# The gated delta-rule stage of a decoder kernel: gating and output projection in the next slot, late formings on two pairs of banks, compactions between exponentials

## The chip, the cores and the metric

The kernel runs as one program on one core of a Trainium2 chip. A core has TensorE (PE; its weight loads are PEld), VectorE (DVE), ScalarE (ACT), GpSimd (POOL) and SyncE (SP), each with its own instruction queue, which it works through in order; they meet through semaphores. TensorE writes PSUM, eight banks of 512 floats on 128 partitions. The metric is the time of the whole kernel in microseconds on the device.

## The reference

A decoder of four layers over x of 16 sequences, 128 tokens, 256 channels. All the change touches is the first sublayer: a gated delta rule with 8 heads, each in 8 modes, key and value width 64.

```python
q, k, v = (x @ Wq), (x @ Wk), (x @ Wv)              # 8 heads of 64
beta, tg = sigmoid(x @ Wbeta), sigmoid(x @ Wtg)     # one per head and mode
g = log(clip(tg * rho, 1e-6))                       # rho from log_decay
# q and k are rotated, with frequencies per head and mode, and normalised
def step(S, (q_t, k_t, v_t, b_g, b_beta)):          # over the 128 tokens
    S = S * exp(b_g)
    dv = (v_t - k_t S) * b_beta
    S = S + k_t^T dv
    return S, q_t S
o = sum over modes of softmax(mode_logits) * step outputs
o = o * sigmoid(x @ Wg)
x = layernorm(x + o @ Wo)
```

## The kernel before

The stage is `delta_stage`. A **slot** g is one of the 16 sequences. It has two **units**, u = 2g (heads 0 to 3, hf 0) and u + 1 (heads 4 to 7, hf 1). A unit is 32 combinations of head and mode, in eight groups of four. The recurrence is solved in matrix form: decayed products of keys with keys and queries (`NB`, 128 x 128 for each combination), the inverses of their 32 x 32 diagonal blocks, and three block couplings.

The steps of a unit, by function:

- *Rotation* (`rotate`, VectorE, two multiplications for each half; `add_halves`, GpSimd) makes `kq` for a pack of two groups.
- *Exponents* (`phase`, TensorE, in bank 0), *exponential* (`decays`, ScalarE, into `NB`), *products* (`phase`, TensorE, banks 4 and 5 for even groups, 1 and 2 for odd), *multiplication* (`take_products`, VectorE). These run over eight groups: "the phase of a unit".
- *Compaction* (`take_lower`, ScalarE): the diagonal blocks of `NB` into `diagonal`. *Inversion* (`invert`, VectorE): a transposition, 60 small dependent operations, a transposition. In gaps between these operations other steps of VectorE are put, by a list of positions. *Spreading* (`spread`, ScalarE): the inverses into the block diagonal `Df`.
- *Forming* (`form`, TensorE, banks 6 and 7) multiplies a group of `NB` by `Df`; `take_formed` (ScalarE, four copies) takes it back. Eight a unit: two of them inside the next unit's phase, six after it. *Identities* (`set_identities`, ScalarE) prepare the next unit's diagonal blocks.
- *Couplings* (`couple`, q = 1, 2, 3; four heads each, 16 small matmuls a head, into banks 4 to 7) and *solutions* (`solutions`, ScalarE); *output* (`output`, TensorE, bank 3).
- *Gating* (`gated`, VectorE) multiplies the output of a unit by the gates of the slot; after both, the *output projection* (`project_out`, TensorE, bank 3) and, in the next slot, sum and normalisation (`finish`, `applied`).

Each engine's order is written out by hand in its `turn(g, ...)`: slot 0 and slot 15 straight, slots 1 to 14 as a hardware loop (`Fori`). A slot's queue on each engine goes: phase of the odd unit with the first formings of the even one; late formings, couplings and output of the even unit, with the q, k, beta and decay projections of slot g + 1 in between; phase of the next slot's even unit; late formings, couplings and output of the odd unit, with the v projection and the gates' projection of slot g + 1. In VectorE's queue gating stands ahead of the phase:

```python
invert(u + 1, between(*sorted(steps, key=lambda x: x[0])))
gated(g, 0)
if more:
    phase(g + 1, u + 2, 0)
    invert(u + 2)
gated(g, 1)
```

After this stage come eleven others, which the change leaves alone.

## Time and profile before

| | |
|---|---|
| median of 3 runs | 6994.44 us (6984.17 to 7002.9) |
| the profiled execution, its own time | 7007.31 us |
| its span in the trace | 7005.5 us |
| granted TensorE clock, mean | 0.836 of full |
| delta-rule stage | 0 to about 2605 us of the span |
| the 14 middle slots | about 153.5 us each, some 157 |

In the rows below a timeline line is: start in us, duration in us, engine, line of the code, operation, what it writes and reads, how many instructions are merged in it, and in brackets the idle time of the engine before it with what ended it ("issue": nothing that the profile shows). A windows line is: the stretch, its length, the busy us of PE, PEld, DVE, ACT and POOL with the number of instructions, the granted clock as a share of 2.4 GHz, the share of DMA, GB/s.

### The profile page before, as it was taken

What the parts mean: (1) busy time and instruction counts of PE and PEld (TensorE: products, weight loads), DVE (VectorE), ACT (ScalarE), POOL (GpSimd) and SP (SyncE); (2) the same over time, 40 slices, a digit from 0 to 9 for tenths busy, and PEclk for the clock granted to TensorE, in tenths of its full rate; (3) what the DMA queues carried; (4) which work ended last, traced back from release to release, by engine and by line L of the source; (5) the groups of instructions that cost most, each with busy time, mean ns of one, the idle gap of its engine ahead of it and who ended that gap; (6) DMA issues with size and microseconds to landing.
All of it is one profiled execution on the core that took longest, in us unless ns stands there. A gap on an engine that the chain in (4) does not pass through costs nothing. (4 is left out here: it accounts for less than half of the span.)

```text
span 7005.5 us, 79394 instructions
## 1 busy us (share of the span) xinstructions
PE 5363.7 (77%) x28132; PEld 3704.0 (53%) x28132; DVE 3454.2 (49%) x7576; ACT 2207.6 (32%) x3719; POOL 1034.3 (15%) x845
## 2 busy tenths in 40 slices
PE   3778778777777775899998877547768567788698
PEld 1556556555655663566665555323446235565454
DVE  6566666566666634100003554548834445544444
ACT  2455454545544531121211222321113322232111
POOL 1221221222122113000001222100001002222000
PEclk8898898889988887799999878755568677788799
DMA  0000000000000000000000000000000000000000
GB/s 31 1 1 1 1 1 1 2 1 1 1 1 1 1 13 9 35 24 12 24 12 7 0 24 10 12 3 0 0 33 0 5 4 4 21 6 1 9 18 25
DMA packets 13502, 63.23 MB, mean 9 GB/s; under 512 B 1168, under 2 KB 5648, under 8 KB 11152
## 3 DMA queue, kind: packets, MB, share of 16 engines
q1 hardware_dynamic: 13200, 59.17, 2.4%
q8 instruction: 193, 3.16, 0.2%
q14 instruction: 109, 0.89, 0.0%
HBM read 57.07 MB, written 2.10 MB: 8 GB/s over the span
## 5 line engine op out<-in xcount | busy, mean ns | idle before, releaser
L1480 PE MATMUL psum<-arena 128*128 128x512 f32 x1600 | 707.1, 596 | 58.4 <-DVE Y L1544 35.8
L808 PE MATMUL psum<-arena 128*128 128x256 f32 x2048 | 526.8, 402 | 176.8 <-ACT arena L1011 175.6
L1561 DVE SCALAR_TENSOR_TENSOR Y<-psum,arena,Y 128x256 f32<-128x256 f32 x416 | 172.5, 477 | 848.0 <-PE psum L1492 848.0
L1492 PE MATMUL psum<-arena 128*128 128x256 f32 x2624 | 583.0, 380 | 4.1 <-DVE arena L1585 4.1
L696 POOL TENSOR_TENSOR arena<-arena 128x512 f32<-128x512 f32 x256 | 331.6, 1315 | 1657.8 <-DVE arena L1179 1657.8
L1492 PEld LDWEIGHTS psum<-arena 128*128 128x128 f32 x2624 | 499.1, 190 | 111.7 <-issue 43.5
L808 PEld LDWEIGHTS psum<-arena 128*128 128x128 f32 x2048 | 385.5, 197 | 307.5 <-ACT arena L1011 223.4
L841 PE MATMUL psum<-arena 64*128 64x256 f32 x2048 | 354.0, 473 | 246.4 <-POOL arena L696 246.4
L1480 PEld LDWEIGHTS psum<-arena 128*128 128x128 f32 x1600 | 304.5, 191 | 409.5 <-issue 341.8
L860 PE MATMUL psum<-arena 64*32 64x64 f32 (+2 forms) x6144 | 520.1, 250 | 0.0
L144 POOL TENSOR_TENSOR arena<-arena,eps 128x4 f32<-128x4 f32 (+2 forms) x76 | 15.0, 197 | 3263.4 <-DVE arena L139 3263.4
L1189 DVE TENSOR_TENSOR arena<-psum,arena 128x1024 f32<-128x1024 f32 x256 | 313.2, 1223 | 308.1 <-PE psum L841 162.7
L860 PEld LDWEIGHTS psum<-arena 64*32 64x32 f32 (+2 forms) x6144 | 448.0, 129 | 12.3 <-issue 6.6
L1526 ACT ACTIVATE arena<-psum,arena 128x512 f32<-128x512 f32 x256 | 175.9, 687 | 701.5 <-PE psum L1480 701.5
L422 PE MATMUL psum<-ident,arena 128*128 128x128 f32 x1280 | 217.2, 325 | 212.7 <-ACT arena L493 212.7
L841 PEld LDWEIGHTS psum<-arena 64*128 64x128 f32 x2048 | 213.1, 225 | 306.9 <-POOL arena L696 144.6
L402 PE MATMUL psum<-arena 128*128 128x512 f32 x640 | 354.0, 686 | 16.8 <-ACT arena L482 11.2
L1223 DVE TENSOR_TENSOR weights<-weights 128x30 f32<-128x30 f32 (+14 forms) x960 | 318.7, 332 | 33.0
L414 PEld LDWEIGHTS psum<-arena 128*128 128x128 f32 x2048 | 280.9, 214 | 100.9 <-issue 60.3
L1222 DVE TENSOR_TENSOR weights<-weights 128x30 f32<-128x30 f32 (+14 forms) x960 | 318.0, 331 | 30.9
L1009 ACT COPY arena<-psum 128x512 f32<-128x512 f32 x256 | 150.1, 586 | 497.9 <-PE psum L808 497.2
L422 PEld LDWEIGHTS psum<-ident,arena 128*128 128x128 f32 x1280 | 178.5, 171 | 234.9 <-ACT arena L493 234.7
(434 smaller groups left out, 9010.5 us busy)
## 6 DMA issues: line engine op xcount, KB each, us to landing
arena<-in_experts_L_ffn SPq DMA_DIRECT2D x8, 2052.0 KB, 8.4
arena<-in_ctxT SPq DMA_DIRECT2D x16, 512.0 KB, 3.3
arena<-in_experts_L_ffn SPq DMA_DIRECT2D x18, 384.0 KB, 3.1
weights<-in_w_L_attn SPq DMA_DIRECT2D x1, 3106.0 KB, 13.5
weights<-in_w_L_ffn SPq DMA_DIRECT2D x1, 3072.0 KB, 9.8
weights<-in_w_L_ffn SPq DMA_DIRECT2D x1, 2753.0 KB, 10.7
weights<-in_w_L_relu SPq DMA_DIRECT2D x1, 2436.0 KB, 8.9
X<-in_x SPq DMA_DIRECT2D x1, 2048.0 KB, 8.1
```

The costliest lines, as they stand in the source:

```text
L402: mm = nc.tensor.matmul(out[:, b * 4:b * 4 + 4, :], qT[:, c, u * P:(u + 1) * P], km[:, at % 2, b * 4:b * 4 + 4, :], start=True, stop=True)
L414: mm = nc.tensor.matmul(o_psum[:, c * HH + h, :], pT[:, j % 2, h, :], v, start=True, stop=True)
L422: mm = nc.tensor.transpose(pt_psum[:, h, :], pr[:, j % 2, h, :], k.ident[:, :])
L696: pool.tensor_tensor(both_, both_, t1[:, j, :, :], ALU.add).then_inc(s["rotated"], 1)
L808: mm = nc.tensor.matmul(ps[:, 6 + j // 2, (j % 2) * 2 * P:(j % 2 + 1) * 2 * P], Df[:, c, :], both(hf)[:, :, c, :], start=True, stop=True)
L841: mm = nc.tensor.matmul(ps[:, bank, m * 2 * P:(m + 1) * 2 * P], kq[rows, i // 2 % 2, at, 0, :], kq[rows, i // 2 % 2, at, :, :], start=True ...
L860: mm = nc.tensor.matmul(ps[n:n + Q, 4 + h, m * DK:(m + 1) * DK], NB[0:n + Q, 2 * (u_odd), place(h, m), n:n + Q], ur[0:n + Q, h, m, :], sta ...
L1189: dve.tensor_tensor(both(hf)[:, :, group, :].rearrange("p k c t -> p c k t"), products, bc(NB[:, 2 * hf + 1, group, :], 2, 2), ALU.mult).t ...
L1222: linked(dve.tensor_tensor(part, bc(inv[:, j + 1:, j], 2, j), bc(inv[:, j, 0:j], 1, below), ALU.mult))
L1223: linked(dve.tensor_tensor(inv[:, j + 1:, 0:j], inv[:, j + 1:, 0:j], part, ALU.add))
L1480: mm = nc.tensor.matmul(ps[:, bank, :], W[s][name][:, c, f * P:(f + 1) * P], xT[:, g, c, :], start=(c == 0), stop=(c == C - 1))
L1492: mm = nc.tensor.matmul(out, h[:, m % 2, f, u * P:(u + 1) * P], W[s]["w2"][:, f, :], start=(f == 0), stop=(f == FC - 1))
```

## The change

1. Gating of a unit moves on VectorE from its place after the output to behind the first pack of the next phase (`phase(..., gate=...)`). The output projection of slot g moves on TensorE into the odd phase of slot g + 1, after its fifth group (only slot 15 keeps it at the end).
2. The first two pairs of rotations of the odd unit's phase move into the inversion of the even unit before it (positions 40 and 46).
3. The gates are projected in their own slot, after the odd phase, into bank 0, and taken by ScalarE (`take_gates`) right after the compaction; before, this was done for slot g + 1 at the end of slot g, in bank 1.
4. Formings with i = 3, 5 and 7 go to banks 4 and 5, so that those from i = 4 on wait for the copies of the one before the last instead of the last. The wait for the phase's last products moves from the first coupling to the forming i = 3.
5. The compaction of the first half of the groups is cut in two, one part before the exponential of group 6 and one after it. The identities move behind the copies of forming i = 5. `take_x` and `turn_x` come after the gates.
6. The sums of logarithms (`sum_logs`) come before the turning of q and k, one coupling earlier; ScalarE's `round_sums` and `round_rest` with them. Positions in VectorE's inversion change by two or so.

```diff
@@ TensorE @@
             def turn_x(g):
                 pe.wait_ge(s["x_staged"], g + 1)
-                need(pe, "decay_ready", g * HALVES * GROUPS)
+                need(pe, "gates_ready", g)
...
-            def project_gates(g, products):
-                pe.wait_ge(s["swapped_ready"], (g + 1) * 2)
-                need(pe, "products_taken", products)
+            def project_gates(g):
+                pe.wait_ge(s["decay_ready"], (g + 1) * HALVES * GROUPS)
                 for co in range(PAIRS):
                     for c in range(C):
-                        mm = nc.tensor.matmul(ps[:, 1, co * P:(co + 1) * P], ...
+                        mm = nc.tensor.matmul(ps[:, 0, co * P:(co + 1) * P], ...
...
-            def form(u, hf, i):
+            def form(u, hf, i, products=None):
 
                 if i == 0:
                     pe.wait_ge(s["inverse_ready"], u + 1)
                     need(pe, "solution_ready", u * (NQ - 1) * HALF)
+                elif i < 4:
+                    pe.wait_ge(s["couplings_formed"], u * GROUPS + i)
                 else:
-                    pe.wait_ge(s["couplings_formed"], u * GROUPS + i)
+                    pe.wait_ge(s["couplings_formed"], u * GROUPS + i - 1)
+                if i == 3 and products is not None:
+                    pe.wait_ge(s["products_taken"], products)
+                at = 4 if i in (3, 5, 7) else 6
...
@@ TensorE, turn @@
                     if i in (2, 5):
                         form(u, 0, i // 3)
+                    if i == 4 and (not isinstance(g, int) or g):
+                        project_out(g - 1)
+                project_gates(g)
+                form(u, 0, 2)
                 if more:
                     turn_x(g + 1)
-                form(u, 0, 2)
-                form(u, 0, 3)
+                form(u, 0, 3, (u + 1) * GROUPS + GROUPS - 1)
...
-                couple(u, 0, 1, (u + 1) * GROUPS + GROUPS - 1)
+                couple(u, 0, 1)
                 if more:
+                    sum_logs(g + 1)
                     turn_qk(g + 1)
                 couple(u, 0, 2)
                 if more:
-                    sum_logs(g + 1)
                     swap(g + 1)
...
                     if more and i == 4:
                         project_v(g + 1)
-                    if more and i == 6:
-                        project_gates(g + 1, (u + 3) * GROUPS)
...
-                project_out(g)
+                if not more:
+                    project_out(g)
@@ ScalarE, turn @@
-                    if i == 5:
-                        take_lower(u + 1, 1, 0)
+                    if i in (5, 6):
+                        take_lower(u + 1, 1, 0, (2 * i - 10, 2 * i - 9))
+                take_lower(u + 1, 1, 1, range(NQ))
+                take_gates(g)
+                take_formed(u, 0, 2)
                 if more:
                     take_x(g + 1)
-                take_lower(u + 1, 1, 1)
-                take_formed(u, 0, 2)
                 take_formed(u, 0, 3)
...
                 for i in range(5, GROUPS):
                     take_formed(u, 0, i)
+                    if i == 5:
+                        set_identities(u + 1, 1)
                 if more:
                     logarithms(g + 1)
-                set_identities(u + 1, 1)
                 solutions(u, 1)
                 if more:
+                    round_sums(g + 1)
                     take(g + 1, qkT, "qk_turned", "qkT_ready")
+                    round_rest(g + 1)
                 solutions(u, 2)
                 if more:
-                    round_sums(g + 1)
-                    round_rest(g + 1)
                     take(g + 1, qkS, "swapped", "swapped_ready")
...
                 if more:
                     spread(u + 2)
-                    take_gates(g + 1)
@@ VectorE @@
-            def phase(g, n, hf):
-                for j in range(2):
+            def phase(g, n, hf, turned=False, gate=None):
+                for j in range(0 if turned else 2):
                     rotate(g, n, hf, 0, j)
                 for p in range(NPACKS):
+                    if p == 1 and gate:
+                        gate()
...
             def turn(g, first, more):
                 u = g * HALVES
-                phase(g, u + 1, 1)
+                phase(g, u + 1, 1, True, None if first else lambda: gated(g - 1, 1))
...
-                gated(g, 0)
                 if more:
-                    phase(g + 1, u + 2, 0)
-                    invert(u + 2)
-                gated(g, 1)
+                    phase(g + 1, u + 2, 0, False, lambda: gated(g, 0))
+                    invert(u + 2, between((40, lambda: rotate(g + 1, u + 3, 1, 0, 0)),
+                                          (46, lambda: rotate(g + 1, u + 3, 1, 0, 1))))
+                else:
+                    gated(g, 0)
+                    gated(g, 1)
```

## Rows read from the trace of the kernel before

**Rows 1.** Windows: busy us per engine, granted clock (PEclk), the stage's steady part

```profile
313.00:2470.00 2157.00, 1697.07 (x13356) 1274.56 (x13356) 1353.70 (x2730) 1080.80 (x2128) 462.74 (x405) 0.89 0.01 1
```

**Rows 2.** Timeline of VectorE: product multiplications that bound the four legs

```profile
1402.08 1.22 DVE L1189 TENSOR_TENSOR arena<-psum,arena 128x1024 f32<-128x1024 f32 x1 [1.71 <-PE psum L841]
1426.09 1.22 DVE L1189 TENSOR_TENSOR arena<-psum,arena 128x1024 f32<-128x1024 f32 x1 [2.25 <-PE psum L841]
1478.05 1.22 DVE L1189 TENSOR_TENSOR arena<-psum,arena 128x1024 f32<-128x1024 f32 x1 [1.71 <-PE psum L841]
1500.48 1.23 DVE L1189 TENSOR_TENSOR arena<-psum,arena 128x1024 f32<-128x1024 f32 x1 [0.67 <-PE psum L841]
1555.58 1.22 DVE L1189 TENSOR_TENSOR arena<-psum,arena 128x1024 f32<-128x1024 f32 x1 [1.71 <-PE psum L841]
```

**Rows 3.** Timelines of all engines at the edge of two slots

```profile
1549.42 0.38 PE L820 MATMUL psum<-arena 128*128 128x512 bf16 x1 [2.09 <-issue]
1553.46 2.08 PE L841 MATMUL psum<-arena 64*128 64x256 f32 x8 [3.23 <-POOL arena L696]
1541.81 4.20 ACT L1045 COPY arena<-weights 32x1024 f32<-32x1024 f32 x4
1544.85 0.42 DVE L1233 SCALAR_TENSOR_TENSOR arena<-psum,arena 128x256 f32<-128x256 f32 x1 [14.53 <-PE psum L875]
1547.89 0.69 DVE L1174 TENSOR_TENSOR arena<-arena,weights 128x512 f32<-128x512 f32 x1 [2.61 <-issue]
```

**Rows 4.** Timelines of TensorE and ScalarE: formings, projections, couplings

```profile
1432.86 3.60 PE L748 MATMUL psum<-weights 128*128 128x512 f32 x8
1448.78 0.16 PE L734 MATMUL psum<-arena 128*128 128x1 bf16 x1 [1.19 <-issue]
...
1508.55 1.99 PE L808 MATMUL psum<-arena 128*128 128x256 f32 x8 [1.14 <-ACT arena L1011]
1510.38 1.88 PE L787 MATMUL psum<-weights 128*128 128x512 f32 x4
1511.07 0.57 ACT L1011 COPY arena<-psum 32x128 f32<-32x128 f32 x3
1521.75 3.15 ACT L1036 COPY arena<-ident 32x1024 f32<-32x1024 f32 x3
```

**Rows 5.** Timelines inside the even phase: GpSimd, ScalarE, TensorE, VectorE

```profile
1486.78 2.49 POOL L696 TENSOR_TENSOR arena<-arena 128x512 f32<-128x512 f32 x2 [3.74 <-DVE arena L1179]
1495.33 2.54 ACT L1027 ACTIVATE weights<-arena 32x512 f32<-32x512 f32 x4
1495.56 1.13 PE L841 MATMUL psum<-arena 64*128 64x256 f32 x8 [0.69 <-POOL arena L696]
1498.59 1.22 DVE L1189 TENSOR_TENSOR arena<-psum,arena 128x1024 f32<-128x1024 f32 x1 [4.53 <-ACT arena L1019]
```

**Rows 6.** Timelines of VectorE and ScalarE in the second half of leg B

```profile
1460.89 0.75 DVE L1281 SCALAR_TENSOR_TENSOR arena<-arena,weights,psum 128x512 f32<-128x512 bf16 x1 [4.43 <-ACT arena L988]
1471.27 1.28 ACT L1019 ACT_TABLE_LOAD   x1
1472.57 0.60 ACT L1019 ACTIVATE arena<-psum 128x512 f32<-128x512 f32 x1
```

**Rows 7.** TensorE in slots 0 and 8, then windows over leg D's end

```profile
205.31 0.16 PE L734 MATMUL psum<-arena 128*128 128x1 bf16 x1 [1.19 <-issue]
230.34 3.71 PE L875 MATMUL psum<-arena 128*64 128x128 f32 x64
...
1466.26 3.71 PE L875 MATMUL psum<-arena 128*64 128x128 f32 x64
1525.84 1.91 PE L860 MATMUL psum<-arena 64*32 64x64 f32 x16
...
1525.00:1537.00 12.00, 12.00 (x107) 10.89 (x106) 4.91 (x13) 4.42 (x8) 0.00 (x0) 0.50 0.01 1
1539.00:1551.00 12.00, 8.62 (x112) 7.24 (x111) 3.52 (x6) 9.66 (x11) 0.54 (x1) 1.00 0.02 5
```

More of the change, by code:

```diff
@@ L844, in phase, with couple @@
                 mm.then_inc(s["products_ready"], 1)
-            def couple(u, u_odd, q, products=None):
+            def couple(u, u_odd, q):
                 n = q * Q
@@ L853, in couple @@
                         pe.wait_ge(s["identities_set"], u + 1)
-                        if h == 0 and products is not None:
-                            pe.wait_ge(s["products_taken"], products)
                     else:
@@ L918, in turn @@
                 for i in range(2, GROUPS):
-                    form(u + 1, 1, i)
+                    form(u + 1, 1, i, (u + 2) * GROUPS + GROUPS - 1 if more and i == 3 else None)
                     if more and i == 4:
                         project_v(g + 1)
-                    if more and i == 6:
-                        project_gates(g + 1, (u + 3) * GROUPS)
-                couple(u + 1, 1, 1, (u + 2) * GROUPS + GROUPS - 1 if more else None)
+                couple(u + 1, 1, 1)
                 couple(u + 1, 1, 2)
@@ L1001, in take_gates @@
                 need(act, "o_gated", g * HALVES)
[L1002 removed]
+                nc.scalar.activation(gateT[:, :, :], ps[:, 0, :].rearrange("p (c t) -> p c t", t=P), ACT.Sigmoid
                                      ).then_inc(s["gates_ready"], 1)
@@ L1020, in decays, with take_lower @@
                                      ACT.Exp).then_inc(s["decay_ready"], 1)
-            def take_lower(n, hf, x):
+            def take_lower(n, hf, x, quarters):
                 act.wait_ge(s["products_taken"], n * GROUPS + 4 * (x + 1))
-                for q in range(NQ):
+                for q in quarters:
                     rows = slice(q * Q, (q + 1) * Q)
-                    a = nc.scalar.activation(diagonal[rows, 16 * x:16 * (x + 1), :], NB[rows, 2 * hf, 16 * x:16 * (x + 1), rows],
-                                             ACT.Copy, scale=-1.0)
-                a.then_inc(s["lower_taken"], 1)
+                    nc.scalar.activation(diagonal[rows, 16 * x:16 * (x + 1), :], NB[rows, 2 * hf, 16 * x:16 * (x + 1), rows],
+                                         ACT.Copy, scale=-1.0).then_inc(s["lower_taken"], 1)
             def set_identities(n, hf):
-                act.wait_ge(s["lower_taken"], (n + 1) * 2)
+                act.wait_ge(s["lower_taken"], (n + 1) * 2 * NQ)
                 for q in range(1, NQ):
@@ L1092, in turn @@
                         take_formed(u + 1, 1, i // 3)
-                    if more and i == 5:
-                        take_lower(u + 2, 0, 0)
+                    if more and i in (5, 6):
+                        take_lower(u + 2, 0, 0, (2 * i - 10, 2 * i - 9))
                 if more:
-                    take_lower(u + 2, 0, 1)
+                    take_lower(u + 2, 0, 1, range(NQ))
                 for i in range(2, GROUPS):
@@ L1100, in turn @@
                         take_v(g + 1)
-                if more:
-                    set_identities(u + 2, 0)
+                    if more and i == 5:
+                        set_identities(u + 2, 0)
                 solutions(u + 1, 1)
@@ L1119, in _ @@
                 decays(0, 0, i)
-                if i == 5:
-                    take_lower(0, 0, 0)
-            take_lower(0, 0, 1)
+            take_lower(0, 0, 0, range(NQ))
+            take_lower(0, 0, 1, range(NQ))
             set_identities(0, 0)
             take_v(0)
-            take_gates(0)
             spread(0)
@@ L1299, in turn @@
                 u = g * HALVES
-                phase(g, u + 1, 1)
+                phase(g, u + 1, 1, True, None if first else lambda: gated(g - 1, 1))
                 state = {}
-                def between(*steps):
-                    out = []
-                    for at, step in steps:
-                        out += [None] * (at - len(out)) + [step]
-                    return out
                 def remember(key, f):
@@ L1318, in turn, with between @@
                 if more:
[L1319 to L1323 removed]
+                    steps += [(16, lambda: sum_squares(g + 1)), (22, lambda: scale_decays(g + 1)),
+                              (24, lambda: clip_decays(g + 1)), (32, lambda: normalise(g + 1)),
+                              (38, remember("views", lambda: split(g + 1))),
+                              (40, lambda: split_rest(g + 1, state["views"])),
+                              (52, lambda: first_part(g + 1)), (58, lambda: second_part(g + 1))]
                 if not first:
                     steps += [(2, remember("ch", lambda: finish(g - 1))), (14, applied)]
[L1326 to L1327 removed]
+                invert(u + 1, between(*steps))
                 if more:
[L1329 to L1331 removed]
+                    phase(g + 1, u + 2, 0, False, lambda: gated(g, 0))
+                    invert(u + 2, between((40, lambda: rotate(g + 1, u + 3, 1, 0, 0)),
+                                          (46, lambda: rotate(g + 1, u + 3, 1, 0, 1))))
+                else:
+                    gated(g, 0)
+                    gated(g, 1)
+            def between(*steps):
+                out = []
+                for at, step in sorted(steps, key=lambda x: x[0]):
+                    out += [None] * (at - len(out)) + [step]
+                return out
             sum_squares(0)
@@ L1340, in _ @@
             phase(0, 0, 0)
-            invert(0)
+            invert(0, between((40, lambda: rotate(0, 1, 1, 0, 0)), (46, lambda: rotate(0, 1, 1, 0, 1))))
             turn(0, True, True)
```

20 lines of the change are left out of this document (5 added, 15 removed).

## The prediction

> **What bounds the kernel now.** I read a table of windows, then the timelines of all engines over one slot of the delta-rule stage. The stage fills the first 2605 us of 7005.5; the later stages are untouched. In its steady part TensorE, the busiest engine, works 1697 of 2157 us, VectorE 1354, ScalarE 1081: even the busiest waits a fifth of the time [rows 1]. What sets the time is a chain that passes between engines, and the timelines show who waits for whom in it.
>
> I cut a slot of 153.5 us by VectorE's product multiplications, first and last of each phase [rows 2]. Leg A, the odd phase: 1402.08 to 1427.31, 25.23 us. Leg B, to the first product of the even phase (late formings, three couplings, output): 1427.31 to 1478.05, 50.74. Leg C, the even phase: 23.66. Leg D, to the next slot's first product: 1501.71 to 1555.58, 53.87. What ends last in each is what the change has to move.
>
> **Leg D, slot start.** (I count the eight formings of a unit from 1; the first two lie in the phase.) Before: the output ends at 1544.8, gating waits for it, the projection waits for gating, TensorE then idles 2.09 us at the loop's edge, VectorE 2.61; rotations begin after that, GpSimd adds the halves, and the first product's matmuls wait 3.23 for it [rows 3]. From output to first multiplication: 10.8 us. After: the projection and gating are gone from here, and the first rotations lie in the inversion before, under the 14.53 us in which VectorE waits for the output [rows 3] (four operations of 0.69 us, 2.8 us: free; without that cover 2.8 a slot). What is late next is TensorE itself: its loop edge, 2.09, exponents 0.8 (two of 0.38 and four short matmuls, overlapped), and product matmuls 1.1, so 4.0 us after the output. ScalarE's spreading (4.20 us) ends 1.2 after the output, inside those 4.0. Gain 6.8.
>
> Ahead of it lie the formings. Before, one takes 1.99 us and the next waits 1.14 for its copies, 3.13 a forming; coupling starts 20.1 us into the leg, as the last copies end at 1521.75 [rows 4]. After, on two pairs of banks, only forming 4 waits for its predecessor's copies (it starts at 3.7 us, as now); then 1.83 a forming (1508.55 to 1510.38, back to back), with the v projection (1.88 us) at 7.4, so that forming 6 starts at 9.2. The identities (3.15 us of ScalarE) now come after forming 6's copies, ahead of those of 7 and 8: copies end at 12.2, identities at 15.3, the last two copies (1.05 each) at 17.4. Coupling starts at 17.5: gain 2.6, and ScalarE bounds it. Leg D: 53.87 - 6.8 - 2.6 = 44.5.
>
> **Legs A and C, the phases.** A pack of two groups takes 6.2 us, GpSimd's 2.5 us and 3.7 of its waiting for VectorE [rows 5]: multiplication, rotation, halves, matmuls. This loop is not touched. But the seventh group waits for its exponential, held up by 2.54 us of compaction [rows 5]. Split in halves around the exponentials, half stays ahead: I get the last group done 22.1 us after the first where it was 23.66 (gain 1.55). Gating (0.42) goes between two multiplications where VectorE has about that much slack. In the odd phase the projection (1.99) now sits in TensorE's queue ahead of the sixth group's exponents, the second forming and the seventh group's exponents; exponents, copies and compaction each move by up to 1.8, and the end comes at 23.95 instead of 25.23 (gain 1.3).
>
> **Leg B.** ScalarE's order after the phase is now compaction 2.57, a table load 1.28, the gates' sigmoid 0.60, only then the copies of the third forming, at 4.5 us, ending at 5.55. TensorE then: forming 4 at 5.6, qk projection 3.6 us at 7.4, forming 5 at 10.9, bt, forming 6 at 13.05, forming 7 at 14.8, forming 8 at 16.6. ScalarE: copies until 16.05, identities until 19.2, two copies until 21.3. Coupling starts at 21.4; before it was 1448.78 - 1427.31 = 21.5 [rows 2, 4]. So double banks save here what gates and identities cost: nothing is left. The gates' projection on TensorE (as many columns as a forming, so about 2 us) is free, since ScalarE is compacting then. From 21.4 TensorE is back to back through couplings, sums, turns, swap (17.5 us) and output (3.7), done at 42.4 (42.7 before). VectorE, before, ended its inversion at 1467.02 after a 4.43 us wait for rounded sums [rows 6]; sums now come one coupling earlier, that wait goes, and the inversion ends at 35.3. It could rotate at once; GpSimd is ready at 40.4. What is late is ScalarE: last solutions 39.35, spreading 4.2, exponential table 1.28, exponential 0.6 [rows 6]: first product at 45.5 instead of 50.74. Gain 5.2, all of it from starting rotations ahead of gating.
>
> On the table load the trace shows 1.28 us and the next activation some 20 ns behind its end [rows 6]. The Trainium skill (ScalarE: Activation LUTs, What ACT_TABLE_LOAD costs) gives 2.66 us for a switch of sets, with a drain; an estimate by it makes leg B 1.4 us longer, some 20 us over the stage. No row here shows that drain. Loads per slot go from five to three, by my reading of the order of functions (sigmoid twice in succession, exponentials across the loop's edge); if the loop's head keeps a load, leg D hides it (0.7 us to spare), and a second sigmoid load would cost at most 1.28 a slot.
>
> **Sum at full clock.** 23.95 + 45.5 + 22.1 + 44.5 = 136.05, a gain of 17.45 a slot.
>
> **The clock.** In leg D the couplings run at the lower of the clock's two levels, 1.2 GHz, from about the third head on, and for over 12 us: a granted clock of 0.50 with TensorE busy all the while, 1.91 us a head [rows 7]. At the higher level (2.4 GHz) a head takes 1.08, and twelve heads 13.4 us; here they take 19.3 (1521.8 to the output's start at 1541.1), so this fall costs 5.9, which I left in leg D. In leg B the same couplings run at full clock in the slot shown, but in slot 0 the stretch from first coupling to output took 25.0 us where 17.5 is usual: there the fall came too, after the same pattern of formings [rows 4, 7]. After the change TensorE idles 2.8 us ahead of the couplings in both legs (forming 8 ends at 18.55, coupling at 21.4; 14.7 and 17.5). Where the falls seen came after gaps of 1.1 us, a gap of 2.8 makes one likelier in leg B. The price of one is 5.9 (what the even half pays) to 7.5 (slot 0, 25.0 - 17.5); I take 6.5, between them. The phases too may see a slow stretch after GpSimd's wait; before they had one of some 6 us each, which I left out of A and C; I allow 1.0 a slot for both (between 0 and 2, if the matmuls of a group or two take 2.08 instead of 1.13 [rows 3, 5]). Slot: 136.05 + 6.5 + 1.0 = 143.5, gain 10.0.
>
> The Trainium skill (TensorE: Matmul & The Clock Gate, Part 1: The HAM clock gate) says that the clock follows how busy the engine was lately and that only sustained work releases it. The half clock after idle gaps agrees; that it stays low for over 12 us of a busy engine [rows 7] the rule does not explain. By it the longer gap ahead of the couplings takes part of the gain back, which is the case I forecast, at the price of the rows.
>
> **Ends.** Fifteen slots have both halves: 15 x 10.0 = 150. The last slot gains leg A's 1.3 and five of the 1.14 waits between its last formings, and some in the odd formings; the prologue loses one gates' projection and sigmoid: 12 together, between 0 and 20 (an estimate from the rows above). Total 162: the profiled execution's 7007.31 becomes 6845. The runs' median lies 12.9 below that execution, so I predict 6832.
>
> **Rivals.** (1) The clock holds in leg B: 17.45 x 15 + 12 = 274, 6720. For it: odd couplings kept full clock in all slots shown after the first. Against: the longer gap. (2) The leg B fall comes in every slot, with slot 0's price, and ScalarE's new order (gates, identities ahead of copies) costs 3 us more a slot than I read, by a second load and by copies that queue behind the square: gain 17.45 - 7.5 - 2 - 3 = 4.95, total 86, 6908. (3) The change does not do what it says: the chain through GpSimd and the loop edge stays, as the rotations ahead wait on a semaphore that I misread; only the formings' 2.6 and the phases' 2.85 stay, less 6.5 for the clock: 1.05 x 15 = 16 lost, 12 gained, 6998. (4) Slower: the clock falls ahead of the couplings and stays at the lower level until the phase is over. In leg B the 17.5 us of couplings and turns and the 3.7 of output then take about 1.8 times as long (1.91 over 1.08), 17 us more; in leg D the four heads that are fast now and the output add 3.3 + 3.0; the two phases, at 2.08 instead of 1.1 for a group's matmuls, some 3. Loss 26.3 against the gain of 17.45, so 8.85 a slot worse: 6994 + 8.85 x 15 - 12 = 7115; it decides from 17.45 + 12/15 = 18.25 lost a slot. Against it: in leg D the clock came back under couplings, before the output (1.00 from 1539 on [rows 7]).
>
> **How the numbers follow.** Forecast 0.50, (1) 0.22, (2) 0.20, (3) 0.04, (4) 0.04. A difference under 0.3%, about 21 us, is what measurement cannot tell from none. The range reaches from (1) to (2), which leaves out (3), (4) and the outer edges of both: 6715 to 6910. Faster: 0.50 + 0.22 + 0.20 = 0.92; same 0.04, case (3); slower 0.04, case (4).
>
> **What would show it.** Right: the projection behind the fifth group's products; no idle "issue" ahead of the rotations; first product 4 us after the output in the odd half; ScalarE spreading last before the even phase; forming pitch 1.8 with a gap of 2.8 before coupling; 48 to 64 table loads in this stage. Leg B's couplings at 1.91 confirm the clock term, at 1.08 rival (1). Wrong: coupling later than 21.4 after the odd phase, or an untouched 10.8 from output to product.

## The result, and the profile after

The changed kernel takes 6913.55 us (median of 3 runs, 6906.36 to 6926.08) against 6994.44: a ratio of 0.9888, 95% interval 0.9856 to 0.9919. That is 81 us faster. Forecast were 6832 and a range of 6715 to 6910: the direction was right, the gain half of what was forecast, and the time 4 us outside the range.

First the windows view over the steady part of the stage (columns as in [rows 1]):

```profile
313.00:2400.00 2087.00, 1756.33 (x13299) 1370.36 (x13298) 1357.88 (x2720) 1047.11 (x2096) 458.23 (x403) 0.85 0.01 1
```

TensorE is busy 84% of this stretch where it was 79% [rows 1], for the same work in each slot, and the granted clock fell from 0.89 to 0.85. Over the whole kernel its busy time grew from 5363.7 to 5430.9 us. More busy time for the same work is the first thing to see: the clock took part of the gain back.

Then the leg ends, as in [rows 2], on VectorE's timeline:

```profile
1354.18 1.22 DVE L1189 TENSOR_TENSOR arena<-psum,arena 128x1024 f32<-128x1024 f32 x1 [15.79 <-PE psum L843]
1378.12 1.22 DVE L1189 TENSOR_TENSOR arena<-psum,arena 128x1024 f32<-128x1024 f32 x1 [0.70 <-PE psum L843]
1432.52 1.23 DVE L1189 TENSOR_TENSOR arena<-psum,arena 128x1024 f32<-128x1024 f32 x1 [4.58 <-ACT arena L1021]
1453.72 1.23 DVE L1189 TENSOR_TENSOR arena<-psum,arena 128x1024 f32<-128x1024 f32 x1 [0.70 <-PE psum L843]
1504.19 1.23 DVE L1189 TENSOR_TENSOR arena<-psum,arena 128x1024 f32<-128x1024 f32 x1 [14.07 <-PE psum L843]
```

Leg A is 25.16 us (25.23 before), leg B 53.2 (50.74), leg C 22.4 (23.66), leg D 49.25 (53.87). Slots vary; the means over the 14 looped slots (1 to 14), read off the same timelines, are the better figures:

| mean us | A | B | C | D | slot |
|---|---|---|---|---|---|
| before | 25.2 | 50.7 | 23.7 | 54.5 | 154.1 |
| forecast (its own base 153.5) | 23.95 | 52.0 with the clock's 6.5 | 22.1 | 44.5 | 143.5 with 1.0 for the phases |
| after | 24.6 | 52.5 | 23.0 | 49.9 | 149.95 |

The slot's edge, which answers to [rows 3], on TensorE, ScalarE and VectorE:

```profile
1495.86 3.71 PE L875 MATMUL psum<-arena 128*64 128x128 f32 x64
1502.26 0.38 PE L824 MATMUL psum<-arena 128*128 128x512 bf16 x1 [2.69 <-issue]
1503.01 1.14 PE L843 MATMUL psum<-arena 64*128 64x256 f32 x8
...
1496.58 4.21 ACT L1046 COPY arena<-weights 32x1024 f32<-32x1024 f32 x4
...
1489.44 0.68 DVE L1179 TENSOR_TENSOR arena<-arena,Y 128x512 f32<-128x512 f32 x1
```

The chain is what was forecast: no gating, projection or rotation is left behind the output (the last rotations ran at 1489), ScalarE's spreading ends at 1500.8, and the first multiplication comes 4.6 us after the output's end where it came 10.8. Only the loop's edge is longer: 2.69 us here and 2.8 on average over the stage (2.45 to 3.11), where it was 2.09 in [rows 3] and 2.0 on average (1.71 to 2.28).

The formings and couplings of leg D answer to [rows 4]. TensorE and ScalarE:

```profile
1458.68 5.41 PE L812 MATMUL psum<-arena 128*128 128x256 f32 x16 [3.12 <-ACT arena L1013]
1465.64 5.34 PE L812 MATMUL psum<-arena 128*128 128x256 f32 x24
1473.94 0.16 PE L734 MATMUL psum<-arena 128*128 128x1 bf16 x1 [2.95 <-issue]
1474.03 1.91 PE L860 MATMUL psum<-arena 64*32 64x64 f32 x16
1493.63 1.18 PE L860 MATMUL psum<-arena 128*32 128x64 f32 x16
...
1468.65 3.15 ACT L1037 COPY arena<-ident 32x1024 f32<-32x1024 f32 x3
1471.83 0.59 ACT L1011 COPY arena<-psum 128x512 f32<-128x512 f32 x1
```

Here is the loss. Forming 4 starts 3.74 us into the leg, as forecast, after 3.12 us of idling, but formings 4 and 5 take 5.41 us together instead of the forecast's 3.8: part of them runs at the lower clock. In eight of the 14 looped slots they take 6.6 to 6.7 us, the lower clock throughout. The gap itself is old; in the kernel before it stood ahead of the same forming:

```profile
1505.41 1.99 PE L808 MATMUL psum<-arena 128*128 128x256 f32 x8 [3.05 <-ACT arena L1011]
```

The identities (3.15 us) stand ahead of the last two copies; TensorE waits 2.95 us for these, and then the couplings start at the lower clock (1.2 GHz) from the first head: 1.91 us a head for ten heads, where the same slot before the change had six, and two that were slow in part.

Leg B, ScalarE and then TensorE:

```profile
1381.98 1.28 ACT L1003 ACT_TABLE_LOAD   x1
1383.28 0.60 ACT L1003 ACTIVATE arena<-psum 128x512 f32<-128x512 f32 x1
1383.77 0.58 ACT L1011 COPY arena<-psum 128x512 f32<-128x512 f32 x1
1430.52 1.28 ACT L1021 ACT_TABLE_LOAD   x1
...
1384.86 3.56 PE L812 MATMUL psum<-arena 128*128 128x256 f32 x8 [0.43 <-ACT arena L1013]
1402.15 0.16 PE L734 MATMUL psum<-arena 128*128 128x1 bf16 x1 [2.95 <-issue]
1402.25 1.91 PE L860 MATMUL psum<-arena 64*32 64x64 f32 x16
1416.03 1.08 PE L860 MATMUL psum<-arena 96*32 96x64 f32 x16
```

The gates' load and sigmoid, then the copies of forming 3, 4.4 us into the leg (forecast 4.5). Forming 4 takes 3.56 us here, where a forming at full clock takes 1.99. The couplings start after the same 2.95 us gap, 22.8 us in, and four heads run at 1.91, where leg B had none before the change in slots 1 to 14.

The two couplings in the windows view, leg B's and leg D's:

```profile
1402.00:1425.00 23.00, 22.84 (x220) 20.06 (x221) 15.92 (x42) 11.43 (x20) 0.49 (x1) 0.71 0.01 2
1474.00:1496.00 22.00, 22.00 (x206) 19.93 (x208) 14.24 (x30) 6.51 (x12) 2.60 (x2) 0.55 0.01 2
```

The granted clock was 0.71 and 0.55, with TensorE busy throughout. In the looped slots couplings to output now take 22.1 to 23.4 us in leg B (17.45 before, in every one of the 14) and 20.7 to 22.1 in leg D (19.24).

### The profile page after: what moved, and what is told of

It is laid out like the page before. It is cut to its first block and busy times, and to the rows that moved or that the text cites. A ratio compares the mean times of both kernels' runs of the same rounds, so it can differ in the third digit from the quotient of the medians.

```text
span 6924.3 us, 79364 instructions
## 1 busy us (share of the span) xinstructions
PE 5430.9 (78%) x28132; PEld 3808.8 (55%) x28132; DVE 3468.1 (50%) x7576; ACT 2177.9 (31%) x3691; POOL 1032.2 (15%) x845
## 3 DMA queue, kind: packets, MB, share of 16 engines
q8 instruction: 180, 2.95, 0.2%
## 5 line engine op out<-in xcount | busy, mean ns | idle before, releaser
L812 PE MATMUL psum<-arena 128*128 128x256 f32 x2048 | 559.8, 430 | 60.8 <-ACT arena L1013 59.6
L860 PE MATMUL psum<-arena 64*32 64x64 f32 (+2 forms) x6144 | 596.9, 272 | 0.0
L1496 PE MATMUL psum<-arena 128*128 128x256 f32 x2624 | 583.0, 380 | 4.1 <-DVE arena L1589 4.1
L1496 PEld LDWEIGHTS psum<-arena 128*128 128x128 f32 x2624 | 499.3, 190 | 111.8 <-issue 43.5
L1484 PEld LDWEIGHTS psum<-arena 128*128 128x128 f32 x1600 | 304.4, 191 | 409.1 <-issue 341.4
L812 PEld LDWEIGHTS psum<-arena 128*128 128x128 f32 x2048 | 429.4, 216 | 179.1 <-ACT arena L1013 74.5
L860 PEld LDWEIGHTS psum<-arena 64*32 64x32 f32 (+2 forms) x6144 | 517.5, 144 | 13.9 <-issue 7.8
L843 PE MATMUL psum<-arena 64*128 64x256 f32 x2048 | 298.7, 411 | 129.2 <-POOL arena L696 129.2
L1225 DVE TENSOR_TENSOR weights<-weights 128x30 f32<-128x30 f32 (+14 forms) x960 | 335.0, 349 | 33.5
L1224 DVE TENSOR_TENSOR weights<-weights 128x30 f32<-128x30 f32 (+14 forms) x960 | 331.0, 345 | 31.0
L1053 ACT ACTIVATE arena<-psum 32x512 f32<-32x512 f32 x384 | 226.2, 589 | 377.0 <-PE psum L860 376.4
L414 PEld LDWEIGHTS psum<-arena 128*128 128x128 f32 x2048 | 284.8, 217 | 101.6 <-issue 61.5
L300 POOL TENSOR_TENSOR arena<-arena,weights 128x1024 f32<-128x1024 f32 x128 | 242.3, 1901 | 407.4 <-PE psum L402 341.7
```

The lines of the kernel that those rows point to most:

```text
L414: mm = nc.tensor.matmul(o_psum[:, c * HH + h, :], pT[:, j % 2, h, :], v, start=True, stop=True)
L812: mm = nc.tensor.matmul(ps[:, at + j // 2, (j % 2) * 2 * P:(j % 2 + 1) * 2 * P], Df[:, c, :], both(hf)[:, :, c, :], start=True, stop=True)
L843: mm = nc.tensor.matmul(ps[:, bank, m * 2 * P:(m + 1) * 2 * P], kq[rows, i // 2 % 2, at, 0, :], kq[rows, i // 2 % 2, at, :, :], start=True ...
L860: mm = nc.tensor.matmul(ps[n:n + Q, 4 + h, m * DK:(m + 1) * DK], NB[0:n + Q, 2 * (u_odd), place(h, m), n:n + Q], ur[0:n + Q, h, m, :], sta ...
L1224: linked(dve.tensor_tensor(part, bc(inv[:, j + 1:, j], 2, j), bc(inv[:, j, 0:j], 1, below), ALU.mult))
L1225: linked(dve.tensor_tensor(inv[:, j + 1:, 0:j], inv[:, j + 1:, 0:j], part, ALU.add))
```

## The experiments

Times are medians; ratios are to the kernel before, measured in the same round as the variant: 6998.0 us for the first four variants, from "identities last" to "one pair of banks"; 7004.9 for "gating in place", "two pairs alone", "D's couplings filled" and "forming gaps filled"; 6999.0 for the other three. The changed kernel itself was measured only in the round of the result, so where two variants of different rounds are compared, some 10 us of the difference may be the round. **Fillers** are matmuls whose result nobody reads; they change no output:

```python
def filler(bank, n):
    for _ in range(n):
        nc.tensor.matmul(ps[:, bank, :], ident_h, later_h[:, :, :], start=True, stop=True)
```

| kernel | us | ratio, 95% interval | slot | B: start, length of couplings | D: start, length |
|---|---|---|---|---|---|
| before | 6994 | 1 | 154.1 | 21.6, 17.5 | 21.1, 19.2 |
| after | 6914 | 0.9888 (0.9856 to 0.9919) | 149.95 | 23.0, 22.6 | 19.8, 21.9 |
| identities last | 6713 | 0.9587 (0.9562 to 0.9611) | 136.1 | 20.4, 20.8 | 17.1, 14.4 |
| both gaps filled | 6698 | 0.9568 (0.955 to 0.9587) | 136.0 | 21.3, 18.6 | 17.4, 15.9 |
| gap ahead of couplings filled | 6786 | 0.9688 (0.9665 to 0.9711) | 140.9 | 22.5, 19.5 | 19.5, 16.7 |
| one pair of banks | 6978 | 0.9971 (0.9961 to 0.9981) | 153.9 | 26.2, 21.1 | 22.7, 20.7 |
| gating in place | 7023 | 1.003 (1.0019 to 1.0041) | 156.8 | 21.6, 23.2 | 18.7, 20.6 |
| before, two pairs alone | 6902 | 0.9848 (0.9828 to 0.9869) | 150.8 | 18.1, 21.6 | 18.3, 18.4 |
| before, D's couplings filled | 6975 | 0.9964 (0.9952 to 0.9975) | 152.1 | 21.8, 22.3 | 21.1, 13.4 |
| before, both legs' filled | 6913 | 0.9883 (0.9866 to 0.99) | 149.2 | 22.2, 17.5 | 21.6, 13.4 |
| identities last, whole compaction | 6775 | 0.9693 (0.9676 to 0.9711) | 139.4 | 20.9, 21.2 | 16.1, 13.9 |
| identities last, forming gaps filled | 6691 | 0.9558 (0.954 to 0.9576) | 133.1 | 19.6, 20.3 | 15.7, 13.9 |
| identities last, all gaps filled | 6619 | 0.9463 (0.9449 to 0.9477) | 129.7 | 19.6, 18.5 | 15.7, 13.4 |

Starts are counted from the end of the phase, lengths from the first head to the end of the last; both are means in us over the looped slots.

**Identities last.** One part of the change undone, in both legs (the cut shows the even unit's):

```diff
                     take_formed(u, 0, i)
-                    if i == 5:
-                        set_identities(u + 1, 1)
                 if more:
                     logarithms(g + 1)
+                set_identities(u + 1, 1)
...
```

> The changed kernel with the identities behind all eight copies again, as before the change. Theory (a), ScalarE's order holds the couplings up: identities (3.15 us) stand ahead of the last two copies, so couplings start 3.15 us earlier in both legs, 6.3 a slot, 94 us over fifteen slots; the solutions wait for the identities but TensorE still has the first coupling to run (4.45 us and more). If the clock also holds because the idle gap ahead of the couplings shrinks from 2.95 to some 0.5 us, up to 8 us a slot more, 215 together: 6700 to 6820. Rival (b), the couplings' small matmuls bring the clock down whatever stands ahead: only the 94 us, and the heads still at 1.91 us, 6820. Rival (c), solutions or GpSimd wait instead: no change, 6914.

6713 us: 200 less than the changed kernel, much more than the 94 of the earlier start. Leg D's couplings in one slot: the gap ahead of them, the first head and the last (TensorE's timeline):

```profile
1217.61 0.16 PE L734 MATMUL psum<-arena 128*128 128x1 bf16 x1 [1.19 <-issue]
1217.71 1.08 PE L860 MATMUL psum<-arena 64*32 64x64 f32 x16
1230.01 1.08 PE L860 MATMUL psum<-arena 128*32 128x64 f32 x16
```

The gap is 1.19 us instead of 2.95, and all twelve heads run at 1.08, as they do in 12 of the 14 looped slots of leg D. Leg B still has slow heads in 11 of 14. Starts came 2.6 and 2.7 us earlier; the shorter couplings gave 1.8 in B and 7.4 in D: the clock's share is the larger one. Rival (b), which allowed only the 94 us, is out.

**Gaps filled, order kept.** This separates clock from order: the identities stay where the change put them, and TensorE gets more to do.

```diff
                 form(u, 0, 2)
+                pe.wait_ge(s["products_taken"], (u + 2) * GROUPS)
+                filler(1, 8)
...
+                if more:
+                    pe.wait_ge(s["bt_ready"], g + 2)
+                    filler(0, 12)
                 couple(u, 0, 1)
...
+                    if more and i == 3:
+                        pe.wait_ge(s["products_taken"], (u + 3) * GROUPS)
+                        filler(1, 13)
                     form(u + 1, 1, i, ...)
...
+                if more:
+                    pe.wait_ge(s["v_ready"], g + 2)
+                    filler(0, 12)
                 couple(u + 1, 1, 1)
```

> The changed kernel with useless matmuls (128x512 bf16, 0.22 us each at full clock) on TensorE in the gap ahead of forming 4 (8 in leg B, 13 in leg D) and in the gap ahead of the couplings (12 in each leg). Theory (a), the idle gaps bring the clock down: formings in leg D back at 1.99 us, couplings at 1.08 for most heads, 22 to 18 us a unit in both legs; 8 us a slot or 120 in all, 6795. Rival (b), the small matmuls of the couplings do it: the clock falls inside the couplings as before the change (19.3 us a unit), gain at most 2.7 a unit or 60 in all, 6850 to 6914. Rival (c), filling costs as much as it gives (fillers run at half clock and delay the couplings): 6914 or above.

> As the run with both gaps filled, but only the gap ahead of the couplings (12 useless matmuls in each leg). Theory (a): leg B, where the formings run at full clock, gets couplings of 17.5 to 19; in leg D the clock has fallen already ahead of forming 4, so that the 12 fillers take 5.2 us there, 2.3 more than the gap, but bring the clock back: about even there, 50 us gained in all, 6860. Rival (b): couplings fall as they did, 6914 to 6950.

6698 and 6786 us: 216 and 128 less than the changed kernel, for work that nobody needs. The expected 120 and 50 were too small; the direction is what theory (a) says, and both times lie outside the ranges of (b) and (c). With the second gap alone filled leg D still starts with formings at half clock, and its couplings start 19.5 us in; with both filled they start at 17.4, the forecast's 17.5.

But the fillers did not end the falls. With both gaps filled the couplings still have slow heads in 5 of 14 slots of leg B and in 6 of 14 of leg D; the six take 19.24 us, as leg D's did before the change; with the second gap alone filled it is 9 and 8 of 14. One such slot of leg D, both gaps filled (TensorE's timeline):

```profile
2163.38 2.75 PE L753 MATMUL psum<-arena 128*128 128x512 bf16 x12
2166.49 0.16 PE L734 MATMUL psum<-arena 128*128 128x1 bf16 x1 [0.36 <-issue]
2167.70 1.08 PE L864 MATMUL psum<-arena 64*32 64x64 f32 x16
2170.14 1.91 PE L864 MATMUL psum<-arena 64*32 64x64 f32 x16
```

In the 13 us ahead of these couplings TensorE is never idle for longer than 0.36 us, and the clock falls all the same, in the third head. So idle time ahead is not all of the cause: the fall inside the couplings that rival (b) describes is still there in part of the slots.

**One pair of banks.** The forming's banks back to 6 and 7 for every i, and the wait on the group before; the rest of the change stays.

```diff
-                elif i < 4:
-                    pe.wait_ge(s["couplings_formed"], u * GROUPS + i)
                 else:
-                    pe.wait_ge(s["couplings_formed"], u * GROUPS + i - 1)
+                    pe.wait_ge(s["couplings_formed"], u * GROUPS + i)
...
-                at = 4 if i in (3, 5, 7) else 6
+                at = 6
```

> The changed kernel with all formings on banks 6 and 7 again, each waiting for the copies of the one before (3.13 us a forming). My sums: without the second pair the identities and the gates are not paid for: leg B's couplings start about 24.6 to 26 us into the leg instead of 22.9, leg D's 22.5 to 23.3 instead of 19.1 to 20.3; some 5.5 us a slot, 83 in all, so about 6995, no better than before the change. Rival: the shorter gap ahead of the couplings (1.2 instead of 2.95 us) lets the clock hold, which returns 3 to 8 us a slot: 6880 to 6950.

6978, outside the rival's range and 17 us below the 6995 expected: couplings start 3.2 and 2.9 us later, and their length shrinks by 1.5 and 1.2 us. The gap right ahead of them is down to 1.19 us, yet both legs still have slow heads in all 14 slots. The wait for the identities has only moved: TensorE now idles 2.2 to 2.3 us ahead of the last forming.

**Two pairs alone, on the kernel before.** Only the banks and the waits of `form`, and the same in `take_formed`:

```diff
-                else:
+                elif i < 4:
                     pe.wait_ge(s["couplings_formed"], u * GROUPS + i)
+                else:
+                    pe.wait_ge(s["couplings_formed"], u * GROUPS + i - 1)
+                if i == 3 and products is not None:
+                    pe.wait_ge(s["products_taken"], products)
+                at = 4 if i in (3, 5, 7) else 6
```

> The kernel before with the two pairs of banks alone; gates, identities, gating and projection stay where they were. By the sums of the prediction formings go from 3.13 to 1.83 us: couplings 4.5 us earlier in leg D (no identities ahead of the last copies) and about 4 in leg B: 8 a slot, 120 in all, 6875, if the clock stays as it is. Theory (a): with formings denser and the gap ahead of the couplings still 1.2 us or less the clock does not get worse and may hold in leg D: down to 6790. Rival: in leg B it is not the couplings but ScalarE that is last, so only leg D gains: 6930.

6902, 27 us above the 6875 expected: starts came 3.4 and 2.8 us earlier instead of some 4 and 4.5, and the clock did not stay as it was. Leg B's couplings, at full clock in all 14 slots before, have slow heads in 10 and take 21.6 us on average. Even so this one edit gives as much as the whole change. Everything else together, with the identities' place among it, gives 20 us without the second pair, and nothing that can be measured on top of it.

**Gating in place.** VectorE's gating and first rotations back at their old places:

```diff
-                phase(g, u + 1, 1, True, None if first else lambda: gated(g - 1, 1))
+                phase(g, u + 1, 1)
...
+                gated(g, 0)
                 if more:
-                    phase(g + 1, u + 2, 0, False, lambda: gated(g, 0))
-                    invert(u + 2, between((40, ...), (46, ...)))
+                    phase(g + 1, u + 2, 0)
+                    invert(u + 2)
+                gated(g, 1)
```

> The changed kernel with VectorE's gating back ahead of the phases and the first rotations back behind the output (the projection stays in the next slot's phase). By the prediction's sums the path from output to first product grows from 4.6 to some 9.5 in leg D and from 6.9 in leg B (of which 2.9 are ahead of the first matmuls of the phase) to some 9: 5 + 2 a slot, 105 us in all, 7020. Rival: the clock term takes the difference up, since a later phase starts from the same fall: 6914 to 6960.

7023, as expected: last head to first product 14.25 us instead of 8.2 in leg D, 11.7 instead of 6.9 in leg B. The gain of this part is real: the slot grows by 6.8 us, about 100 us over the stage.

**The kernel before, with fillers.** If idle time next to the couplings costs clock, it did so before the change too. First leg D alone, then both legs:

```diff
+                if more:
+                    pe.wait_ge(s["bt_ready"], g + 2)
+                    filler(0, 5)
                 couple(u, 0, 1, (u + 1) * GROUPS + GROUPS - 1)
...
+                if more:
+                    pe.wait_ge(s["v_ready"], g + 2)
+                    filler(0, 5)
                 couple(u + 1, 1, 1, (u + 2) * GROUPS + GROUPS - 1 if more else None)
```

> The kernel before the change with 5 useless matmuls (1.1 us at full clock) in the 1.19 us gap ahead of the couplings of leg D, nothing else. Theory (a), idle time next to the small matmuls makes the clock fall: couplings of leg D at 1.08 us a head, 13.4 instead of 19.3, 5.9 a slot, 88 us in all: 6910, as much as the whole change gave. Rival (b), thirteen microseconds of small matmuls bring it down by themselves: 6998, unchanged, or some us more for the wait on the copied v.

6975, 65 us short of theory (a). Leg D does what it says: 13.4 us in all 14 slots, never a slow head. But leg B, which nobody touched, falls in 9 of 14 slots, and takes 25.0 us in each. TensorE in one slot of this kernel, leg B without and leg D with fillers (5 matmuls, of which the record holds 4):

```profile
1264.83 0.16 PE L734 MATMUL psum<-arena 128*128 128x1 bf16 x1 [1.19 <-issue]
1266.04 1.65 PE L864 MATMUL psum<-arena 64*32 64x64 f32 x16
1267.73 1.91 PE L864 MATMUL psum<-arena 64*32 64x64 f32 x16
1277.35 1.91 PE L864 MATMUL psum<-arena 96*32 96x64 f32 x16
...
1344.31 1.03 PE L753 MATMUL psum<-arena 128*128 128x512 bf16 x4
1345.54 1.08 PE L864 MATMUL psum<-arena 64*32 64x64 f32 x16
1355.61 1.08 PE L864 MATMUL psum<-arena 128*32 128x64 f32 x16
```

Leg B's gap of 1.19 us was there before the change and cost nothing in slots 1 to 14, but did in slot 0 [rows 7]. The same gap may or may not come with the fall.

> The kernel before with 5 useless matmuls in the 1.2 us gap ahead of the couplings in both legs; with those in leg D alone leg D's couplings ran at full clock in all slots (13.4 instead of 19.2 us), but leg B's, untouched and at full clock before, fell to 22.3 on average. Theory (a): the gap is what lets the clock fall, here as there: 17.5 in leg B too, 148 us a slot instead of 154.4, 6900. Rival (b): the fall only wanders, it comes somewhere in each slot: 6950 to 6990.

6913 (0.9883): ten useless matmuls a slot make the kernel before as fast as the change did. Couplings take 17.45 and 13.4 us in every slot, and the gap ahead of them is down to 0.11 us. Rival (b), by which a fall comes somewhere in each slot and the time stays above 6950, is out. Some of the gain is lost elsewhere: leg C grows from 23.7 to 24.7 us on average, and leg D's couplings start at 24.1 us instead of 20.2 in 5 slots, where it was 3.

**The best version.** Late identities with fillers, first ahead of forming 4 only, then in all gaps (5 ahead of each leg's couplings as above, and 8 in each phase while TensorE waits for GpSimd):

```diff
                 mm.then_inc(s["exponents_ready"], 1)
+                if i == 2:
+                    filler(6, 8)
                 pe.wait_ge(s["rotated"], (n * NPACKS + i // 2 + 1) * 2)
```

> Identities behind all copies (6713 us alone) and the useless matmuls ahead of forming 4 (8 in leg B, 13 in leg D). Theory (a), idle gaps bring the clock down: the fall that remains with late identities lies in the formings of leg B and D after the gap ahead of forming 4 (couplings of 13.4 in leg D start 15.7 or 17.3 us into it); with the gap filled couplings start at 14.3 in D and 18.3 in B, 1 to 2 us earlier each, and leg B's couplings take 17.5 instead of 18.5 to 22: 3 to 6 us a slot, 6625 to 6670. Rival: fillers displace nothing because ScalarE bounds the formings: 6713.

> Late identities, useless matmuls ahead of forming 4 (8 and 13), and now also 5 in the 1.2 us gap ahead of the couplings of both legs and 8 in each phase, in the 2.4 us that its third group's matmuls wait for GpSimd. Theory (a), idle gaps next to weak stretches bring the clock down: leg B's couplings from 20.3 to 17.5 us, forming 1 in leg A from 3.65 to 1.99: 3 to 5 us a slot from 133.1, 45 to 75 in all: 6615 to 6645. Rival (b), leg B's falls come from its couplings, whatever is ahead: 6691.

6691 and 6619. The first is 21 us above its range: leg B's couplings, still behind a gap of 1.19 us, take 20.3 us. The second lies in its range. With that gap filled too leg B's couplings take 18.5 us, without a slow head in any slot, so the rival by which its couplings fall whatever is ahead is out here, and the windows view shows TensorE at full clock through the stage, first the changed kernel, then this one, over the same stretch:

```profile
313.00:2200.00 1887.00, 1586.86 (x12013) 1235.36 (x12013) 1228.75 (x2454) 947.43 (x1895) 419.37 (x370) 0.86 0.01 1
```

```profile
313.00:2200.00 1887.00, 1708.70 (x14675) 1269.35 (x14674) 1392.58 (x2800) 1079.70 (x2194) 467.07 (x411) 1.00 0.01 2
```

The granted clock is 1.00 instead of 0.86. This kernel beats the one before by 5.4% and the changed one by 4.3%. Leg B stays at 18.5 us and not 17.5, and its trace shows why: between the first and the second coupling TensorE now waits 0.9 us for VectorE (`split_rest`, one of its steps inside the inversion), in every slot.

```profile
1247.15 0.49 PE L767 MATMUL psum<-weights 128*128 128x128 f32 x2 [0.92 <-DVE weights L1295]
```

**Whole compaction**, on the kernel with late identities:

```diff
-                    if i in (5, 6):
-                        take_lower(u + 1, 1, 0, (2 * i - 10, 2 * i - 9))
+                    if i == 5:
+                        take_lower(u + 1, 1, 0, range(NQ))
...
```

> The changed kernel with late identities (6713 us) and the compaction of the first half undivided again. By the prediction's sum the phases lengthen by 1.3 to 1.55 us each, 2.9 a slot, 43 in all: 6756. Rival: the seventh group is held by GpSimd and the rotations anyway: 6713.

6775, 62 us more, where 43 were expected: leg A 26.8 us instead of 24.3, leg C 24.7 instead of 23.2.

**All runs together.** Each profile has 28 couplings in the looped slots. Counted by the idle time right ahead of them, they have slow heads as follows:

| idle time ahead | couplings with slow heads | in |
|---|---|---|
| 0.11 us | 0 of 70 | before with fillers in D, in both legs; all gaps filled |
| 0.36 us | 28 of 56 | both gaps filled; gap ahead of couplings filled |
| 1.19 us | 112 of 182 | before; leg B of before with D filled; all others |
| 2.95 us | 56 of 56 | after; gating in place |

The shorter the gap, the rarer the fall. At 1.19 us all depends on what else there is: none of leg B's 14 in the kernel before, all 28 with one pair of banks (whose other gap, of 2.2 to 2.3 us, stands ahead of the last forming), 2 of leg D's 14 with the identities last. Runs with the same gap differ in their work ahead of it too, so the table shows which way it goes and not a rule.

## Why the prediction was wrong

By its own steps:

- **Slot start (gain 6.8 in leg D, rotations' 5.2 in leg B): right.** Gating in place brings back 6.1 and 4.8 us. TensorE's loop edge and then the first products are last, as forecast; the edge is 0.8 us longer on average.
- **Leg B at 45.5 plus 6.5 for the clock, 52.0: right in the total,** 52.5, with luck in it, as two misses nearly cancel. The couplings start 1.6 us later than the 21.4 of the sum, since forming 4 runs at half clock in whole or in part (with both gaps filled they start at 21.3), and the fall costs 5.2 instead of 6.5 (22.6 against 17.45).
- **Phases (gains 1.3 and 1.55): less than half of it,** 0.5 and 0.7, though the step itself is right: undoing the split costs 2.5 and 1.45. Part of leg A went to forming 1, which runs at half clock in 6 of the 14 slots (3.36 us for 1.99 in the slot shown), an item that the allowance of 1.0 was for.
- **Leg D at 44.5: this step failed.** It is 49.9. The prediction said "this fall costs 5.9, which I left in leg D", and "then 1.83 a forming": it carried the old fall over as it was and ran the formings at full clock. The 3.1 us gap ahead of forming 4 was there before the change too (3.05 us); the 2.95 us gap ahead of the couplings was new. Formings at half clock put the start of the couplings at 19.8 instead of 17.5; a fall from the first head makes them 21.9 instead of 19.25; the edge and the rest give 0.4. That is the missing 5.4 us a slot, most of the 6.4 between 143.5 and 149.95. With both gaps filled the start is 17.4 and the couplings take 15.9: there the loss is gone, and it was the clock.
- The gap of 2.8 us itself was in the prediction, which priced it in leg B alone. The question that it left out is the one that pays: what makes the gap? The identities ahead of the last two copies do. With them behind the kernel takes 6713 us, 119 below the forecast.
- **Rival (1), 6720 with the clock holding in leg B,** did not come: leg B has slow heads in all 14 slots. The kernels with late identities (6713) and with filled gaps (6698) come near its time, but by other sums: couplings have slow heads there in 11 and 5 slots of leg B, and in only 2 and 6 of leg D, where the rival left the old fall as it was. Rival (2), 6908, came nearest in time, by another mechanism: it put 3 us on ScalarE's order and one fall in leg B, where the loss was the clock in leg D. Rivals (3) and (4) are excluded: the rotations do run ahead, and the time is below the one before.
- **Base and ends.** Slot 8 was 153.5 us; the mean looped slot before was 154.1, so a looped slot gained 4.15 us and not 10.0. Over 14 slots that is 82 us less than forecast, against 81 missing in all. Slot 0 gained 17 us where 10 were counted, as its own fall in leg B [rows 7] and a late start in leg D made it 161.8 us long before; the last slot and the prologue gained some 10 of the 12, and the rest, some 4 us, was lost behind the stage.
- **Table loads:** three a slot in the stage in place of five, 48 in place of 80, as read from the order of functions. An estimate by the Trainium skill (ScalarE: Activation LUTs, What ACT_TABLE_LOAD costs) would put the copies behind the gates 1.4 us later than the trace's 4.4. No drain shows in the trace: the load of 1.28 us starts and ends within 20 ns of its neighbours.

What is open is what decides. The same 1.19 us gap costs nothing in leg B of slots 1 to 14 of the kernel before, and comes with a fall in slot 0 and in 9 slots of the kernel with leg D filled; and a gap of 0.36 us still comes with a fall in half of the couplings. In the runs where only 0.11 us was left there was no fall; whether the short gap alone did that, or also the number and kind of fillers, is not shown.

## What to carry to other kernels

When a change takes waits out of TensorE's chain, price the clock anew for every stretch behind a gap that the change makes, moves or leaves; a fall found in the trace of before is no constant of the stage, and it can move to a leg that nobody touched. Then look for what makes the gap: three small copies on ScalarE, moved behind the ones that TensorE waits for, were worth 200 us, more than twice the whole change. And where a gap ahead of small matmuls can't be closed, try to fill it with matmuls that nobody reads, and look in every slot of the trace whether the falls are gone: here 12 of them left the fall in some slots, and 5 that closed the gap to 0.11 us removed it in all.

## What the runs showed of the hardware

- Useless matmuls make a kernel faster: 10 a slot (2.2 us of TensorE) gave 86 us on the kernel before. Behind a gap of 1.2 us, where it fell, the clock went to its lower level within the first three heads and stayed there for 13 to 15 us of small matmuls with no idle time between them (leg D before; leg B with D filled). The Trainium skill (TensorE: Matmul & The Clock Gate, A second HAM failure mode: psum-queue depth-cycling) tells of a kernel in which short idling between groups of matmuls made the clock go up and down; the traces here agree, with 1.91 against 1.08 us a head, as far as falls behind gaps of 1.19 us and more go. With 0.36 us of idling they came in 28 of 56 couplings.
- The fall of one leg depended on the other: filling leg D's gap in the kernel before made leg B, untouched, fall in 9 of 14 slots (17.45 us became 25.0).
- TensorE's loop edge took 1.7 to 2.3 us (13 slots of the kernel before) where the output projection, which waits for VectorE, was last ahead of it, and 2.45 to 3.1 us (13 slots of the changed kernel) where the 64 small matmuls of the output were. That the order makes the difference was not tested by itself.
